# A four-block fp32 transformer kernel: one written list orders the first attention over two batches, eight heads are weighed at a time, and the MEM network begins in the last batch

## The reference

```python
h = rms_norm(layernorm(x)); q, k, v = split(h @ w_qkv)      # 16 heads of 16
q, k = rope(rms_norm(q)), rope(rms_norm(k))
gamma = sigmoid(silu(h @ gg_w1) @ gg_w2)                    # one per batch
w = softmax(q @ k.T * scale, where 0 <= pos_q - pos_k < 64)
attn_out = (w @ v) @ w_o
q_mem = (w * 0.9 ** (pos_q - pos_k) * gamma) @ k
phi = silu(q_mem @ mem_w1); mem_out = (phi + phi ** 2) @ mem_w2
x = x + attn_out * sigmoid(mem_out); x = x + gated_ffn(x)   # MEM, then FFN
# then: a dense FFN with a scaled expert, a latent attention (16 heads), a mixture of 16 experts
```

## Time and profile before

| | before |
|---|---|
| median of 3 runs | 825.58 us (823.99 to 825.9) |
| the profiled execution | 828.07 us, span 826.3 us |
| mean granted clock | 0.905 |
| TensorE busy | 711.1 us (86%), weight loads 567.4 us |
| DVE, ACT, POOL busy | 450.4, 311.2, 261.9 us |
| share of the chain that ended last | PE 66%, DVE 16%, ACT 6%, POOL 4%, DMA 2% |

### The profile page before, as it was taken

One profiled execution on the slowest core, in us unless ns is written; L12 is line 12 of the kernel. 1 busy time (PEld: TensorE's weight loads), 2 busy tenths in 40 slices (PEclk: granted clock), 3 DMA queues, 4 the chain that ended last, 5 costly groups with the idle time before them and its releaser, 6 DMA issues.

```text
span 826.3 us, 12482 instructions
## 1 busy us (share of the span) xinstructions
PE 711.1 (86%) x4880; PEld 567.4 (69%) x4880; DVE 450.4 (55%) x913; ACT 311.2 (38%) x738; POOL 261.9 (32%) x326
## 2 busy tenths in 40 slices
PE   5989976848868869987699999798499999999997
PEld 3665654534557758875577777676388888888886
DVE  5575474747344667655556555654735444544445
ACT  2342333231233324333377677566242222222222
POOL 2232013341152472240542443333512332332310
PEclk9895696957789979998889999999899999999999
DMA  6430000010020210000100000000201111112001
GB/s 208 113 103 25 14 14 8 13 33 21 20 58 21 75 40 20 21 3 17 43 17 2 1 1 2 2 1 2 75 20 39 39 42 55 38 39 58 1 1 52
DMA packets 14235, 27.98 MB, mean 34 GB/s; under 512 B 1856, under 2 KB 5952, under 8 KB 14144
## 3 DMA queue, kind: packets, MB, share of 16 engines
q1 hardware_dynamic: 14176, 27.17, 11.3%
HBM read 24.02 MB, written 1.05 MB: 30 GB/s over the span
## 4 chain that ended last, share of the span: by engine, by line
PE 66%; DVE 16%; ACT 6%; issue 4%; POOL 4%; DMA 2%; SPq 1%; DVEq 0%; ACTq 0%; POOLq 0%
PE ps L624 45%; PE ps L938 3%; PE ps L926 2%; PE ps L736 2%; DVE RD L1429 2%; PE ps L753 2%; PE ps L916 2%; PE ps L632 1%; DVE NB L1273 1%; ACT AO L1208 1%; PE ps L791 1%; PE ps L728 1%; DVE MX L1419 1%; PE ps L646 1%; POOL RM L1743 1%
## 5 line engine op out<-in xcount | busy, mean ns | idle before, releaser
L1791 POOL TENSOR_SCALAR PB<-PB,sml 128x256 f32<-128x256 f32 x128 | 58.8, 478 | 96.0 <-DVE sml L1614 96.0
L624 PE MATMUL ps<-ATh,wh 128*128 128x512 f32 x176 | 72.7, 413 | 7.1 <-POOL wl L1762 2.5
L1125 ACT CAST VVh<-U 128x512 fp32r<-128x512 f32 x50 | 31.0, 620 | 126.3 <-PE ps L624 104.8
L1452 DVE TENSOR_TENSOR U<-U,ps 128x512 f32<-128x512 f32 x50 | 34.3, 687 | 73.3 <-PE ps L624 73.3
L624 PE MATMUL ps<-ATl,wh 128*128 128x512 f32 x176 | 71.2, 404 | 0.0
L624 PE MATMUL ps<-ATh,wl 128*128 128x512 f32 x176 | 70.8, 402 | 0.0
L1760 POOL TENSOR_SCALAR wh<-wr 128x768 fp32r<-128x768 f32 (+3 forms) x31 | 24.0, 773 | 143.9 <-PE ps L624 143.7
L1196 ACT ACTIVATE PB<-ps,sml 128x256 f32<-128x256 f32 x128 | 59.4, 491 | 12.7 <-DVE sml L1608 12.7
L1464 DVE TENSOR_TENSOR VVl<-U,VVh 128x512 fp32r<-128x512 f32 x50 | 40.2, 805 | 36.9 <-ACT VVh L1125 36.9
L1762 POOL TENSOR_TENSOR wl<-wr,wh 128x768 fp32r<-128x768 f32 (+3 forms) x31 | 55.6, 1792 | 2.6
L1208 ACT COPY AO<-ps 128x512 f32<-128x512 f32 x64 | 35.2, 589 | 48.1 <-PE ps L926 48.0
(11 more groups left out here) (290 smaller groups left out, 2088.4 us busy)
## 6 DMA issues: line engine op xcount, KB each, us to landing
wr<-in_w SPq DMA_DIRECT2D x32, 384.0 KB, 3.1
wr<-in_w SPq DMA_DIRECT2D x16, 321.0 KB, 3.0
wr<-in_w SPq DMA_DIRECT2D x11, 256.0 KB, 2.7
XO<-in_x SPq DMA_DIRECT2D x2, 512.0 KB, 4.8
XV<-XF SPq DMA_DIRECT2D x16, 64.0 KB, 1.9
XM<-XF SPq DMA_DIRECT2D x16, 64.0 KB, 2.0
out_dram<-XO SPq DMA_DIRECT2D x8, 128.0 KB, 1.7
wr<-in_w SPq DMA_DIRECT2D x2, 416.0 KB, 6.2
```

Source lines behind the costliest of these rows:

```text
L624: t = x.matmul(o, a, b, start=first and i == 0 and c == 0, stop=last and i == n - 1 and c == 2, skip_group_check=skip)
L1125: x.copy((VV if run == "moe" else HH)[c][0][:, :], b[:, :]).then_inc(*mark("hi", "h", run, j, half))
L1452: x.tensor_tensor(b[:, :], a[:, :], bank("u", run, j, half)[:, :], ALU.mult).then_inc(*vacates("u", run, j, half))
L1791: t = x.tensor_scalar(p[:, c, :], p[:, c, :], m[:, 16 + c:17 + c], 1.0, ALU.mult, ALU.mult)
```

## The change

Four things change together.

1. **Order.** `plan` reads three written lists. An item may carry an engine's letter ("score@p 1 0" is TensorE's part alone), so each engine has its own order. `PERIOD` is repeated for the batches 0 to 2; its first number is the distance to the batch, so that `expo` and `weigh` of b, `turnqk` and `score` of b+1 and `project` of b+2 stand interleaved. QT, KH and KL exist twice. In `PROLOGUE` the scores of batch 0 stand between the `fuse` items. `LAST` holds the last batch with `oproj` and the MEM steps between its `expo` units, and goes on through MEM, FFN, the second block and the first units of the latent attention.
2. **Weighing.** `weigh` takes eight heads: three products (sums, values, decayed keys) in two banks. The operands are zero in 16 of 32 columns (`VZ`, `MK`, `ON`), so that two heads of each strip add up in place. `weighed` needs two reciprocals a batch, and XV and XM are written by DVE; `moved`, XF and VK go.
3. **Masks.** `masked` puts a mask by four matmuls of 64x64 on four quadrants of the array in place of two of 128x128. It needs the masks with their halves swapped (`MS`), made by two DMAs ahead of the load of fuse4.
4. **Banks.** During the prologue the scores use one pair of banks; from `l0begin` two pairs for scores and four banks for the rest; from `l0last` one pair, the other being MEM's sums.

```diff
+PROLOGUE = [
+    "fuse@v 2", "norm1@a 0", "norm1@a 1", "norm1@g 0", "consts", "turn1@p 0", "norm1@v 0", "turn1@a 0", "fuse@v 0",
+    "fuse@p 0", "fuse@p 1", "turn1@v 0", "fuse@a 1", "tables", "clear", "project@p 0", "fuse@p 2", "fuse@v 1",
...
+    "fuse@a 11", "score@p 0 5", "fuse@v 13", "fuse@p 14", "score@v 0 5", "fuse@v 15", "fuse@a 13", "fuse@a 15",
...
+PERIOD = [
+    "expo@a 0 0", "rope@g 2 0", "project@g 2 0", "turnqk@a 1 0", "turnqk@v 1 0", "expo@p 0 0", "rope@v 2 0",
+    "expo@a 0 1", "turnqk@p 1 0", "project@v 2 0", "project@a 2 0", "expo@p 0 1", "rope@g 2 1", "expo@p 0 2",
+    "score@v 1 0", "project@p 2 0", "parted@g -1 1", "score@p 1 0", "turnqk@p 1 1", "turnqk@v 1 1", "expo@a 0 2",
+    "turnqk@a 1 1", "expo@p 0 3", "expo@a 0 3", "project@p 2 1", "score@p 1 1", "project@v 2 1", "score@p 1 2",
+    "weigh@p 0 0", "expo@p 0 4", "expo@p 0 5", "score@v 1 1", "rope@v 2 1", "parted@a -1 1", "score@v 1 2",
+    "project@a 2 1", "score@p 1 3", "headnorm@v 2 0", "project@g 2 1", "score@v 1 3", "weighed@g 0 0", "expo@a 0 4",
+    "weighed@v 0 0", "headnorm@a 2 0", "score@p 1 4", "expo@a 0 5", "score@v 1 4", "parted@a 0 0", "score@v 1 5",
+    "finish@v 2 0", "turnmx@a 1 0", "finish@a 2 0", "finish@a 2 1", "finish@g 2 0", "finish@g 2 1", "finish@v 2 1",
+    "score@p 1 5", "weigh@p 0 1", "parted@g 0 0", "weighed@g 0 1", "turnmx@p 1 0", "weighed@v 0 1",
+]
+LAST = [
+    "expo@a 3 0", "l0last", "expo@p 3 0", "parted@a 2 1", "oproj@p 0", "oproj@a 0", "expo@p 3 1", "expo@a 3 1",
+    "oproj@p 1", "oproj@a 1", "mlpbegin", "step@p mem 0 0", "step@a mem 0 0", "step@v mem 0 0", "expo@p 3 2",
+    "expo@a 3 2", "oproj@a 2", "expo@a 3 3", "oproj@p 2", "oproj@a 3", "oproj@p 3", "parted@g 2 1", "expo@p 3 3",
+    "expo@p 3 4", "weighed@g 3 0", "expo@a 3 4", "weigh 3 0", "parted@a 3 0", "weighed@v 3 0", "expo@a 3 5", "mlpwide",
+    "expo@p 3 5", "step@p mem 1 0", "step@a mem 1 0", "step@v mem 1 0", "parted@g 3 0", "weigh 3 1", "weighed@v 3 1",
+    "weighed@g 3 1", "step@p mem 2 0", "down mem 0 0", "step@a mem 2 0", "step@v mem 2 0", "parted@g 3 1",
+    "down mem 1 0", "parted@a 3 1", "split mem3", "oproj@p 4", "oproj@a 4", "split mem4", "step@v mem 3 0", "oproj@p 5",
+    "oproj@a 5", "step@p mem 3 0", "step@a mem 3 0", "step@v mem 4 0", "step@p mem 4 0", "down mem 2 0", "oproj@p 6",
...
+    for text in PROLOGUE:
...
+    for b in range(3):
+        for text in PERIOD:
+            kind, d, k = text.split()
+            name, d, k = kind.partition("@")[0], int(d), int(k)
+            if b + d > 3 or b + d < 0 or d == 2 and b == 2:
+                continue
+            if name in ("project", "rope", "finish", "turnqk"):
+                item(kind, 2 * (b + d) + k)
+            elif name in ("headnorm", "turnmx"):
+                item(kind, b + d)
+            elif name not in ("weighed", "parted") or b + d >= 0:
+                item(kind, b + d, k)
...
+    for text in LAST:
+        kind, *a = text.split()
+        a = [int(v) if v.isdigit() else v for v in a]
+        order.append((kind, *a))
...
+    MK = (sb("MK0", [128, 2, T]), sb("MK1", [128, 2, T]))
+    VZ = (sb("VZ0", [128, 2, T]), sb("VZ1", [128, 2, T]))
...
+    QT, KH, KL = ([sb(f"{n}{i}", [128, 4, 256], R32, ctx=l0) for i in range(2)] for n in ("QT", "KH", "KL"))
+    MB, MS = (sb(n, [128, 640], BF16, ctx=l0) for n in ("MB", "MS"))
...
-        ring = {"w": Turns((4, 5, 6, 7)), "m": [Turns((0,)), Turns((1,))], "n": Turns((2,))}
+        ring = {"w": Turns((6, 7)), "m": [Turns((2,)), Turns((3,))], "n": Turns((4,)), "S": Turns((8,))}
...
-            ring.update(S=Turns((8, 9)), A=Turns((4, 5)), w=Turns((6, 7)))
+            ring.update(S=Turns((9, 8)), w=Turns((4, 5, 6, 7)))
...
+        def l0last():
+            ring["S"] = Turns((9,))
+        def masked(bk, cols, nf, w_):
+            for i in range(2):
+                for r in range(2):
+                    rs_, c = slice(64 * r, 64 * r + 64), 64 * (r ^ i)
+                    x.matmul(bk[c:c + 64, i, 0:nf * w_], identb[rs_, rs_],
+                             (MS if i else MB)[rs_, cols].unsqueeze(1).to_broadcast([64, nf, w_]), start=True, stop=False,
+                             skip_group_check=True)
 
...
-        def weigh(b, f):
-            bk = fills(ring["A"], "av", b, f)
-            for u in (0, 1, 2 + f // 2 * 2, 3 + f // 2 * 2):
+        def weigh(b, g):
+            for u in (0, 1, 2 + 2 * g, 3 + 2 * g):
                 e.wait_ge(*vacated("st", b, u))
             e.wait_ge(*at("ones"))
             e.wait_ge(*at("v", 2 * b + 1))
             e.wait_ge(*at("vk", 2 * b + 1))
-            for what in range(2):
-                o = 256 if what else 0
+            bd = fills(ring["w"], "ad", b, g)
+            bk = fills(ring["w"], "av", b, g)
+            for what in range(3):
+                to = (bd[:, 0:256], bk[:, 0:256], bk[:, 256:512])[what]
                 for kt in range(2):
-                    q0, q1 = (128, 256) if kt else (0, 192)
-                    for c in range(4):
-                        u = (0 if kt else 2 + f // 2 * 2) + c // 2
-                        p = x.matmul(bk[32 * c:32 * c + 32, o + q0:o + q1], ON[:, :] if what else VK[:, 2 * b + kt, 4 * f + c, :, :].rearrange("p d s -> p (d s)"),
-                                     weights_of(b, u)[:, c % 2, f if kt else f % 2, :], start=kt == 0 and what == 0, stop=kt == 1,
-                                     skip_group_check=True)
-            p.then_inc(*filled("av", b, f))
+                    q = slice(128, 256) if kt else slice(0, 192)
+                    for par in range(2):
+                        for c in range(4):
+                            h = 8 * g + 2 * c + par
+                            f, sp, i = h // 4, h % 4 // 2, h % 2
+                            u = sp if kt else 2 + f // 2 * 2 + sp
+                            mine = (ON[:, 16 - 16 * par:48 - 16 * par], values(2 * b + kt, g)[:, window(h % 8)],
+                                    keys_of(2 * b + kt, h % 8 // 4)[:, g, window(h % 4)])[what]
+                            p = x.matmul(to[32 * c:32 * c + 32, q], mine, weights_of(b, u)[:, i, f if kt else f % 2, :],
+                                         start=kt == 0 and par == 0 and what < 2, stop=kt == 1 and par == 1,
+                                         skip_group_check=True)
+                if what == 0:
+                    p.then_inc(*filled("ad", b, g))
+            p.then_inc(*filled("av", b, g))
...
+        def mlpwide():
+            e.wait_ge(S.sem("free9"), B.used[9])
...
             e.wait_ge(*at("gq", t // 2))
-            x.activation(VK[:, t, :, :, 1], QR[t % 2][:, 16:32, 0, :], ACT.Copy, scale=gq[:, t:t + 1]).then_inc(*mark("vk", t))
+            e.wait_ge(*at("pads", t))
+            for s in range(2):
+                i = x.activation(keys_of(t, s).rearrange("p g (j e) -> p g j e", e=32)[:, :, :, 0:16],
+                                 QR[t % 2][:, 16:32, 0, :].rearrange("p (g s j) d -> p g s j d", g=2, s=2)[:, :, s, :, :], ACT.Copy,
+                                 scale=gq[:, t:t + 1])
...
-            if t >= 2:
-                e.wait_ge(*have("st", t // 2 - 1, 5))
-            x.copy(QT[:, :, ts], bank("tq", t).rearrange("p (f n) -> p f n", f=4)).then_inc(*mark("hi", "tq", t))
+            if t >= 4:
+                e.wait_ge(*have("st", t // 2 - 2, 5))
+            x.copy(QT[t // 2 % 2][:, :, ts], bank("tq", t).rearrange("p (f n) -> p f n", f=4)).then_inc(*mark("hi", "tq", t))
...
-            for k in (4 * b + 2 * g, 4 * b + 2 * g + 1):
-                e.wait_ge(*at("moved", k))
-            e.wait_ge(*have("pv", 2 * b + 1))
+            e.wait_ge(*at("xv", b, g))
             x.copy(BT[0][:, g, bs], XV[:, :]).then_inc(*mark("hv", b, g))
+            e.wait_ge(*vacated("av", b, g))
             x.copy(AT[0][:, g, bs], XM[:, :]).then_inc(*mark("hm", b, g))
 
...
-        def weighed(b, f):
-            k = 4 * b + f
-            u = bank("av", b, f)
-            e.wait_ge(*have("av", b, f))
+        def weighed(b, g):
+            k = 2 * b + g
+            a, before = bank("av", b, g), ((k - 1) // 2, (k - 1) % 2)
+            e.wait_ge(*have("ad", b, g))
             if k:
-                e.wait_ge(*at("rm", k - 1))
-            x.reciprocal(RD[:, :], u[:, 256:512]).then_inc(*mark("rcp", k))
-            e.wait_ge(*at("rm", k))
-            if k >= 2:
-                e.wait_ge(*at("moved", k - 2))
-            x.tensor_tensor(XF[k % 2][:, :], u[:, 0:256], RM[:, :], ALU.mult).then_inc(*vacates("av", b, f))
+                e.wait_ge(*at("rm", *before))
+                e.wait_ge(*at("xv", *before))
+            x.reciprocal(RD[:, :], bank("ad", b, g)[:, 0:256]).then_inc(*vacates("ad", b, g))
+            e.wait_ge(*vacated("ad", b, g))
+            e.wait_ge(*have("av", b, g))
+            if k:
+                e.wait_ge(*at("at", *before))
+            x.tensor_tensor(XV[:, :], a[:, 0:256], RD[:, :], ALU.mult).then_inc(*mark("xv", b, g))
```

(103 more changed lines are left out.)

242 lines of the change are left out of this document (74 added, 168 removed), and 46 rows, old and new, of tables (LAST, PROLOGUE).

## The result

The changed kernel takes **786.53 us**, median of 4 runs (783.35 to 790.17), against 825.5 for the one before (823.99 to 825.9): ratio 0.9533, 95% interval 0.9481 to 0.9584. The forecast was 788. The sum was right, but several of its terms were far off in opposite directions. Medians are of all executions; the ratios and their intervals leave out those over 1.5% above the fastest of the same kernel.

A forecast was written before the change was run, and what follows sets the result against it. The first attention was taken as bound by a circle through all engines at each batch's edge, no engine full. Terms -30.6 - 3 - 2 - 2 + 0 = -37.6 us took the 825.58 median to 788 us, range 760 to 818.

The forecast's parts named there:

- The stage forecast as -33.6: First attention's four batches, 72.1 to 240.1 us: idle time -30.6 us, granted clock -3, weighing against masks 0.
- signs of being wrong: Stage clock far from 0.76, mask units no shorter, TensorE waits of several us each batch, first exp unit after 75 us.
- Order over two batches: First attention: interleaving neighbouring batches removes TensorE's waits at batch edges, idle 12 us in place of 42.6, -30.6 us.
- Clock: First attention: with the long gaps gone, TensorE's granted clock is 0.76 for 0.74, -3 us.
- The rival of a full clock: First attention: clock follows TensorE's busy time, so the filled stage gains 63 us, 759 us in all; chance 0.10.
- Masks: Score and exp units: four quadrant matmuls run at once and halve mask time, -14.1 us in the stage, -2.7 before it.
- slower by the clock: First attention: quadrant masks and spread projection and weighing lower the clock; 817 us at 0.60, 831 at 0.55; chance 0.12.
- Weighing: First attention: 768 records for 512, +14.1 us of TensorE; eight reciprocals, multiplications and the DMAs go, all beside TensorE.
- MEM in the last batch: Last batch: oproj and MEM steps fill exp waits from the single pair of banks; 6 us idle left there.
- It doesn't do what it says: Last batch: MEM waits for split weights and fills nothing, 5 to 8 us more; counted inside the forecast, no separate chance.
- Prologue: Before 72.1 us: shorter masks and less idle time against a later start by turn1 (+3), sum -2 us, between +3 and -6.
- The list behind MEM: Written order from MEM to the latent attention, idle 20.7 us there: -2 us, between +8 and -10.

The follow-up runs named there:

- experiment 1: Changed kernel's new pieces (eight-head weighing, quadrant masks, QT/KH/KL twice) in the order of the kernel before, with its prologue banks: 806.61 us.
- 5: Eight-head weighing and QT, KH, KL twice in the order of the kernel before, with full-array masks: 804.07 us.
- experiment 8: Changed kernel with the prologue in the order of the kernel before, its banks, and batch 0's score units after all fuse items: 786.56 us.
- (2): Kernel before with only its masks changed, to four 64x64 quadrant matmuls: 828.40 us, ratio 1.0001.
- (3): Changed kernel with two full-array mask matmuls per unit in place of the four quadrants: 782.85 us.
- experiment 4: Changed kernel with the four quadrant masks of each unit put twice: 787.43 us.
- experiment 6: Changed kernel with each of the eight reciprocals executed twice, 14 us more of DVE: 805.46 us.
- experiment 7: Changed kernel with MEM and oproj begun only after the last batch's exp and weighing, whose exp units get two pairs of banks: 779.65 us.
- experiment 11: Changed kernel with full-array masks and MEM begun after the last batch: 770.82 us.
- 10: Changed kernel with the order of the kernel before from the FFN network on: 783.06 us.
- 12: Changed kernel with full-array masks, MEM begun after the last batch, and the order of the kernel before from FFN on: 770.11 us.

## Why the prediction was right, by its steps

The time came out right by luck in good part. The stage forecast as -33.6 gave -50.3 in the profiled execution, and the prologue and the list behind, forecast as -4, cost 5.1 and 6.0. Two of the signs of being wrong that the prediction names came true there: a granted clock far from 0.76, and a first exp unit after 75 us. Each step:

- **Order over two batches (-30.6).** Right, and the largest true term: idle 11.4 us for the 12 forecast, to the first sum of MEM, of 45.2 (-33.8). Experiments 1 and 5 share it out otherwise than the text did: 20 us of the idle time go without the new order, with the weighing. The batch's edge was a circle through reciprocal, decay and DMA, and shortening it works in the old order too: TensorE's waits for exp in batches 0 to 2 fall from 22.0 to 14.4 us in experiment 1.
- **Clock (-3).** The step that failed most: "I take 0.76 for 0.74". It was 0.90. The work of some 98 us at full speed (98.2 by the sum above) took 109.5 busy, where 0.76 would have made it 98.2 / 0.76 = 129: 20 us beyond the 3. Over the whole stage the clock gave the 24.3 us above, all of it with the new order, for experiment 1 has 0.78 as before. The rival of a full clock had the direction, but its reason, that the clock follows busy time, does not hold. The Trainium skill, "TensorE: Matmul & The Clock Gate", section Why this matters for your kernels, tells to keep TensorE busy for the full clock; batch 0 of experiment 8 is busy 38.61 of 39.20 us and granted 0.69, batch 2 of the changed kernel 28.72 of 29.80 at 0.77. The trace disagrees: busy time alone doesn't explain the clock; what sets it stays open.
- **Masks (-14.1, and -2.7 in the prologue).** The four quadrants do run together, but a mask takes two thirds, not half. A 384-column mask, from its start to that of the next group, takes 0.28 us in the changed kernel and 0.43 before at full clock; at the lower level 0.47 and 0.75. By the timeline (start, length, instruction), first the changed kernel (57.07 and 61.58 are masks at either level), then the one before (65.31 and 107.84):

```profile
57.07 0.35 PE L690 MATMUL ps<-MB,identb 64*64 64x384 bf16 x2
57.08 0.35 PE L690 MATMUL ps<-MS,identb 64*64 64x384 bf16 x2
57.35 0.47 PE L705 MATMUL ps<-KH,QT 32*128 32x192 f32 x4
61.58 0.53 PE L690 MATMUL ps<-MB,identb 64*64 64x384 bf16 x2 [1.29 <-DVE MX L1426]
62.05 0.74 PE L705 MATMUL ps<-KH,QT 32*128 32x192 f32 x4
```

```profile
65.31 0.82 PE L701 MATMUL ps<-mb,identb 128*128 128x384 bf16 x2
66.06 0.74 PE L707 MATMUL ps<-KH,QT 32*128 32x192 f32 x4
107.84 0.50 PE L701 MATMUL ps<-mb,identb 128*128 128x384 bf16 x2
108.27 0.47 PE L707 MATMUL ps<-KH,QT 32*128 32x192 f32 x4
```

And what it saved did not reach the end: 0 alone (2), 0 or less in the changed kernel (3), and put twice it cost 1 us (4). The rival "slower by the clock" named such a link between masks and clock. I had priced it as a fall of the whole stage, and experiment 4 has a full clock without the full-array form. Whether it is a property of the mask work at all, or of when each batch comes, stays open. With the weighing's +10 us at full speed (14.1 at 0.74) and a third of the masks for a half, the two did not cancel: the stage's work grew by some 6 us at full speed, where the forecast has 0.
- **Weighing (+14.1 on TensorE, DVE and DMA off the path).** The size is right: 34.7 us for 768 records at 0.90, which is 28.18 x 1.5 = 42.3 at 0.74 brought to that clock. "All of it lies beside TensorE in the new order" is wrong: experiment 6 pays 15 to 19 us for 14 of DVE. So the eight reciprocals that went had a price in either order, which the sum had only hidden in the idle time.
- **MEM in the last batch (part of the 6 us idle).** Wrong in sign: with its single pair of banks it costs 7 us or more (7). The rival "It doesn't do what it says" had named it, at 5 to 8 us.
- **Prologue (-2).** 5.1 us later in the profiled execution (and as late, at 77.2 us, in that of experiment 11), some 2 us earlier (69.6 to 70.1 for 72.0) in the profiles of experiments 7, 10, 6 and 12, which have the same order in it. From 60.5 us to its end, in the changed kernel and in experiment 7:

```profile
60.50:77.10 16.60, 15.52 (x53) 9.72 (x54) 8.47 (x28) 1.76 (x7) 7.12 (x8) 0.53 0.27 72
60.50:69.90 9.40, 8.87 (x54) 5.73 (x54) 7.08 (x23) 1.74 (x8) 4.51 (x5) 1.00 0.42 119
```

This may be most of the spread between 783 and 790 us, but one execution of the changed kernel alone was profiled. `turn1` ahead of `fuse` 0 costs a start at 11.91 for 10.13, 1.8 us for the 3 forecast.
- **The list behind MEM (-2).** +5.4 in the profile, of which 3.2 are busy time (98.39 for 95.21, at 0.88 for 0.92) and 2.2 idle; the profile of experiment 10 gives 3 of it back.
- **Sum.** -37.6 forecast, about -39 measured. In the profiled execution the stage gained 16.7 us more than forecast: 21 by the clock and 3 by idle time, less 8 for the work. The prologue came out 7.1 worse and the list and the rest behind it 8.0. That these meet is luck.
